# A new opening for a hypergraph block on one core: warm-up filled by VectorE, W2 prepared along its rows

## What is computed

```
H  = (adj != 0);  w = adj[:, 0, :]
Dn = 1 / (H @ w)          Be = 1 / (column sums of H)
conv(x, W, b) = Dn * (H @ (Be * (H^T @ (x @ W^T)))) + b
h   = relu(conv(x, W1, b1))            # 256 -> 512
h   = layer_norm(h) * gamma + beta
y   = conv(h, W2, b2) + x              # 512 -> 256
out = layer_norm(x + y)
```

## Time and profile before

| | |
|---|---|
| median of 3 runs | 283.41 us |
| profiled execution | 283.37 us, of which the span from first to last instruction is 281.6 us |
| TensorE (PE) busy | 273.6 us, 97% |
| VectorE (DVE) busy | 229.5 us, 82% |
| ScalarE (ACT) busy | 197.3 us, 70% |
| GpSimd (POOL) busy | 136.0 us, 48% |
| granted TensorE clock, mean | 0.995 |

### The profile page before, as it was taken

One profiled execution on the slowest core, in us unless ns is written; L12 is line 12 of the kernel. 1 busy time (PEld: TensorE's weight loads), 2 busy tenths in 40 slices (PEclk: granted clock), 3 DMA queues, 4 the chain that ended last, 5 costly groups with the idle time before them and its releaser, 6 DMA issues.

```text
span 281.6 us, 5797 instructions
## 1 busy us (share of the span) xinstructions
PE 273.6 (97%) x1820; PEld 249.5 (89%) x1820; DVE 229.5 (82%) x648; ACT 197.3 (70%) x561; POOL 136.0 (48%) x199
## 2 busy tenths in 40 slices
PE   7999999999999999999999999999999999999991
PEld 6889889898999989898998989899898989989891
DVE  3795689797878979797897979798897969798884
ACT  3588967776777787777768877676787765574723
POOL 2242546436363644536274553627355353637643
PEclk9999999999999999999999999999999999999998
DMA  6913041335324434432433533443333232110033
GB/s 213 328 55 84 3 130 40 93 113 132 115 57 133 92 93 117 130 114 64 147 72 94 137 109 112 63 147 52 100 91 95 77 113 74 40 57 21 1 112 112
DMA packets 37302, 27.70 MB, mean 98 GB/s; under 512 B 10060, under 2 KB 35352, under 8 KB 37272
## 3 DMA queue, kind: packets, MB, share of 16 engines
q1 hardware_dynamic: 37024, 27.17, 34.0%
q10 hardware_dynamic: 248, 0.17, 0.2%
HBM read 17.21 MB, written 8.42 MB: 91 GB/s over the span
## 4 chain that ended last, share of the span: by engine, by line
PE 90%; ACT 4%; DVE 3%; issue 1%; POOL 1%; POOLq 0%; DVEq 0%; ACTq 0%
PE bank_v L318 31%; PE bank_g L335 10%; PE bank_g L328 10%; PE bank_g L330 10%; PE bank_v L296 9%; PE bank_v L359 8%; PE bank_s L276 4%; PE bank_g L347 3%; PE bank_s L359 1%; PE bank_s L434 1%; ACT ht_sb L533 1%; ACT sq_sb L591 1%; PE bank_g L415 1%; DVE bn_sb L1000 1%; DVE w_lo L844 0%
## 5 line engine op out<-in xcount | busy, mean ns | idle before, releaser
L1049 POOL TENSOR_TENSOR xb_sb<-x_sb,b_half 128x512 f32<-128x512 f32 x32 | 41.2, 1291 | 69.6 <-DVE r_lo L774 50.1
L584 ACT ACTIVATE r_sb<-bank_v,vec 128x512 f32<-128x512 f32 x64 | 44.1, 689 | 39.5 <-PE bank_v L318 38.8
L328 PE MATMUL bank_g<-w_hi,r_hi 128*128 128x258 f32 x256 | 67.0, 294 | 0.0
L330 PE MATMUL bank_g<-w_lo,r_hi 128*128 128x256 f32 x256 | 63.7, 281 | 0.0
L1057 POOL TENSOR_SCALAR r_hi<-r_sb 128x512 fp32r<-128x512 f32 x64 | 44.0, 688 | 39.2 <-ACT r_sb L584 38.7
L318 PE MATMUL bank_v<-u_lo,w_hi 128*128 128x512 f32 x128 | 50.8, 397 | 0.0
L318 PE MATMUL bank_v<-u_hi,w_lo 128*128 128x512 f32 x128 | 50.8, 397 | 0.0
L318 PE MATMUL bank_v<-u_hi,w_hi 128*128 128x512 f32 x128 | 50.7, 396 | 0.0
L328 PEld LDWEIGHTS bank_g<-w_hi,r_hi 128*128 128x128 f32 x256 | 48.3, 189 | 1.7 <-DVE w_lo L844 0.3
L774 DVE TENSOR_TENSOR r_lo<-r_sb,r_hi 128x512 fp32r<-128x512 f32 x64 | 48.7, 782 | 0.9 <-POOL r_hi L1057 0.9
L330 PEld LDWEIGHTS bank_g<-w_lo,r_hi 128*128 128x128 f32 x256 | 48.2, 188 | 1.2
(11 more groups left out here) (127 smaller groups left out, 460.0 us busy)
## 6 DMA issues: line engine op xcount, KB each, us to landing
x_sb<-in_x_dram SPq DMA_DIRECT2D x16, 512.0 KB, 3.9
out_dram<-z_sb SPq DMA_DIRECT2D x14, 512.0 KB, 3.3
adj_sb<-in_adj_dram SPq DMA_DIRECT2D x15, 256.0 KB, 4.1
d_row<-d_rows SPq DMA_DIRECT2D x13, 256.0 KB, 3.5
w_raw<-in_L_gnn_W_dram SPq DMA_DIRECT2D x2, 512.0 KB, 4.8
out_dram<-z_sb SPq DMA_DIRECT2D x3, 256.0 KB, 2.1
adj_sb<-in_adj_dram SPq DMA_DIRECT2D x2, 128.0 KB, 2.3
turned_h<-h_sb SPq DMA_TRANSPOSE x13, 2.4
```

The lines of the kernel that those rows point to most:

```text
L328: pe.matmul(bank_g[:, n, 0:W2COLS], r_hi[:, i % 2, k, graph(n)], w2_hi[:, k], start=(k == 0), stop=False)
L330: pe.matmul(bank_g[:, n, 0:DOUT], r_hi[:, i % 2, k, graph(n)], w2_lo[:, k], start=False, stop=False, skip_group_check=True)
L584: nc.scalar.activation(r_sb[:, k], bank_v[:, k % 2], ACT.Relu, bias=vec[:, k:k + 1]).then_inc(relu_ready, 1)
L1049: nc.gpsimd.tensor_tensor(xb_sb[:, i % 2, part], x_sb[:, i % 3, part], b2_half[:, :].unsqueeze(1).to_broadcast([P, n, DOUT]), ALU.add).the ...
```

## The change

The text of the opening is rewritten; the loop from group 1 on is as before.

1. Warm-up: a tile `warm_b` is filled by VectorE's first instruction, and the warm-up is 22 matmuls of it with itself, which wait for that fill alone. Two more stand behind the first transposes of H, ten ahead of `make_first_s`.
2. W2: gamma comes in as a row for all partitions (a broadcast DMA), not as columns. GpSimd multiplies each half of W2's outputs by it, VectorE centres each half along its row (`bn_stats`, `bn_aggr`, subtract), TensorE turns it, ScalarE and VectorE split it. `scale_w2`, `sum_w2` and `split_w2` in one piece are gone.
3. c2: beta comes in as a row as well; GpSimd multiplies W2 by it, VectorE takes the mean and puts it on a diagonal, and two matmuls of 128 columns with `ones` make c2 in bank_q. This stands late: behind q of group 0 on GpSimd, around `split_u(1)` on VectorE, behind `make_g(0, 3)` on TensorE.
4. `make_g(0, 0)` and `make_g(0, 1)` become `make_first_g`, the two graphs side by side; `make_first_v` does the same with the first two chunks of v; `make_first_u` goes half by half.
5. Orders: x and adj of group 1 are loaded ahead of W2; `turn_q(0)` and `make_u(1)` come behind `make_g(0, 2)`; `make_s(2)` comes behind `make_v(1, 1)`; `make_d(2)`, `make_b(3)`, `add_b2(0, 1)`, `make_htb(3)` and `make_a(2)` move back.

```diff
-KEEP_WARM = 10
+KEEP_WARM = 2
...
             load_x(0)
             load_adj(1)
+            sp.dma_start(gamma_b[:, :], gamma.unsqueeze(0).to_broadcast([P, HID])).then_inc(gamma_in, 16)
+            for c in range(KD):
+                sp.dma_start(w2_raw[:, c], W2[c * P:(c + 1) * P, :]).then_inc(w2_high_in if c else weights_in[2], 16)
             load_adj(2)
             load_x(1)
+            sp.dma_start(beta_b[:, :], beta.unsqueeze(0).to_broadcast([P, HID])).then_inc(beta_in, 16)
...
+            def make_first_g():
+                pe.wait_ge(w2_hi_ready, KD)
+                for n in range(2):
+                    for k in range(KH):
+                        pe.wait_ge(r_hi_ready, k + 1)
+                        add(n, k, r_hi, w2_hi, W2COLS, first=(k == 0))
+                for k in range(KH - 1):
+                    pe.wait_ge(r_lo_ready, k + 1)
+                    for n in range(2):
+                        add(n, k, r_lo, w2_hi, W2COLS)
+                pe.wait_ge(w2_ready, KD)
...
+            def make_c2():
+                pe.wait_ge(diag_ready, KD)
+                pe.wait_ge(at_ready, 2)
                 for c in range(KD):
+                    mm = pe.matmul(bank_q[:, graph(c)], ones[:, :], c2_diag[:, c], start=True, stop=True)
+                mm.then_inc(c2_made, 1)
...
+            pe.wait_ge(warm_ready, 1)
+            keep_warm(WARM_UP)
             pe.wait_ge(consts_ready, 2)
             turn_first_h(0)
+            keep_warm(KEEP_WARM)
+            turn_first_h(1)
             pe.wait_ge(edges_in, 16)
             pe.transpose(bank_g[:, 0, 0:N], edge_rows[:, :], ident[0:N, 0:N]).then_inc(edges_turned, 1)
+            keep_warm(5 * KEEP_WARM)
             make_first_s(0)
+            make_first_s(1)
             turn_w1(0)
+            turn_first_a(0)
             turn_w1(1)
...
+            turn_first_a(1)
+            make_first_u()
+            turn_h(1)
+            make_first_v()
+            make_v(0, 2)
             turn_w2(0)
+            make_v(0, 3)
             turn_w2(1)
             make_s(1)
+            make_first_g()
...
                 make_g(i, 2)
                 if i == 0:
+                    turn_a(1)
+                    turn_h(2)
                     turn_q(0)
+                    make_u(1)
                     make_v(1, 0)
-                    make_s(2)
...
                 if i == 0:
+                    make_c2()
                     make_v(1, 1)
+                    pe.wait_ge(c2_ready, 1)
+                    make_s(2)
                 make_v(i + 1, 2)
                 make_v(i + 1, 3)
...
@@ ScalarE, group 0
             square(0, 3)
+            make_a(1)
+            read_at(1)
+            read_ht(2)
...
                 relu(i + 1, 1)
                 square(i + 1, 1)
                 if i:
                     normalise(i - 1, 0)
+                else:
+                    make_htb(3)
+                    make_a(2)
                 relu(i + 1, 2)
...
@@ VectorE
+            add_squares(0)
             make_h(3)
             make_b(2)
+            sum_beta(0)
 
             for i in range(LAST):
                 split_u(i + 1)
                 if i == 0:
-                    make_b(3)
-                    make_d(2)
+                    sum_beta(1)
...
+                else:
+                    read_c2()
                 read_g(i, 0)
+                if i == 0:
+                    make_b(3)
                 if i + 4 < G:
                     make_h(i + 4)
                 split_r(i + 1, 0)
...
                 read_g(i, 1)
+                if i == 0:
+                    make_d(2)
...
@@ GpSimd
+            for c in range(KD):
+                nc.gpsimd.tensor_tensor(w2_beta[:, c], w2_raw[:, c], beta_b[:, :], ALU.mult).then_inc(beta_scaled, 1)
...
                 split_r(i + 1, 0)
                 if i:
                     inverse_std2(i - 1)
+                else:
+                    add_b2(0, 1)
                 split_r(i + 1, 1)
                 inverse_std1(i, 1)
```

More of the change, by code:

```diff
@@ L340, in make_g, with add @@
                     mm.then_inc(last_g_made, 1)
+            def make_first_g():
+                def add(n, k, r, w, cols, first=False, last=False):
+                    return pe.matmul(bank_g[:, n, 0:cols], r[:, 0, k, graph(n)], w[:, k], start=first, stop=last,
+                                     skip_group_check=True)
+                pe.wait_ge(w2_hi_ready, KD)
[8 more added lines that the diff above has]
+                pe.wait_ge(w2_ready, KD)
+                for n in range(2):
+                    for k in range(KH):
+                        add(n, k, r_hi, w2_lo, DOUT)
+                pe.wait_ge(r_lo_ready, KH)
+                for n in range(2):
+                    mm = add(n, KH - 1, r_lo, w2_hi, W2COLS, last=True)
+                mm.then_inc(g_made, 1)
             def turn_q(i):
@@ L371, in add_last_xb, with keep_warm @@
                     pe.matmul(last_z[n], ident_2[:, :], xb_sb[:, 1, n], start=True, stop=False)
+            def keep_warm(times):
+                for _ in range(times):
+                    pe.matmul(bank_q[:, graph(0)], warm_b[:, :], warm_b[:, :], start=True, stop=True)
             def turn_w1(c):
@@ L377, in turn_w1, with turn_w2 @@
                 mm.then_inc(w1_turned, 1)
-            def turn_w2(half):
-                pe.wait_ge(weights_in[2], 16)
+            def turn_w2(c):
+                pe.wait_ge(w2_centred, c + 1)
                 pe.wait_ge(ht_ready, 1)
[L382 to L385, removed]
+                for k in range(KH):
+                    mm = pe.transpose(w2_turned_in[:, c, k], w2_g[:, c, graph(k)], ident[:, :])
                 mm.then_inc(w2_turned, 1)
@@ L409, in make_first_u @@
                 pe.wait_ge(x_in[0], 16)
-                for c in range(KD):
[L411 to L430, removed]
+                for half in range(2):
+                    for c in range(KD):
+                        if half:
+                            pe.wait_ge(at_ready, 1)
+                        else:
+                            pe.wait_ge(vec_ready if c else edges_ready, 1)
+                        for n in each(half):
+                            mm = pe.matmul(bank_g[:, c, graph(n)], x_sb[:, 0, n, graph(c)], at_sb[:, 0, n],
+                                           start=True, stop=True)
+                        if half:
+                            mm.then_inc(u_made, 1)
@@ new lines, in make_first_v, with add @@
+            def make_first_v():
+                def add(k, c, w, u, first=False, last=False):
+                    return pe.matmul(bank_v[:, k], w[:, c, graph(k)], u[:, c], start=first, stop=last,
+                                     skip_group_check=True)
+                pe.wait_ge(u_hi_ready, 1)
+                for k in range(2):
+                    pe.wait_ge(w1_ready, k + 1)
+                    add(k, 0, w1_hi, u_hi, first=True)
+                    add(k, 0, w1_lo, u_hi)
+                pe.wait_ge(u_lo_ready, 1)
+                for k in range(2):
+                    add(k, 0, w1_hi, u_lo)
+                pe.wait_ge(u_hi_ready, KD)
+                for k in range(2):
+                    add(k, 1, w1_hi, u_hi)
+                    add(k, 1, w1_lo, u_hi)
+                    pe.wait_ge(u_lo_ready, KD)
+                    add(k, 1, w1_hi, u_lo, last=True).then_inc(v_made, 1)
@@ L682, in _ @@
                 if i == 0:
[L683 to L691 removed]
+                    make_htb(2)
+                    read_ht(3)
+                elif i + 3 < G:
+                    make_htb(i + 3)
+                relu(i + 1, 0)
+                square(i + 1, 0)
                 relu(i + 1, 1)
@@ L1096, in _ @@
             pool.wait_ge(consts_ready, 5)
-            for k in range(KH):
-                split_r(0, k)
-            copy_w(2)
             for i in range(LAST):
@@ L1103, in _ @@
                     copy_w(i + 3)
-                for half in range(2):
-                    add_b2(i, half)
+                add_b2(i, 0)
+                if i:
+                    add_b2(i, 1)
                 inverse_std1(i, 0)
```

187 lines of the change are left out of this document (75 added, 112 removed).

## The result

The changed kernel takes **288.15 us** (median of 6 runs, 287.83 to 289.92); the kernel before took 283.40 us in the same comparison (6 runs, 283.37 to 283.72). The ratio is 1.0182 with a 95% interval of 1.0152 to 1.0211: slower by 4.75 us. The forecast was 285.1 us with a range up to 286.2, so the direction was right and the size was not.

The account below looks back on a forecast made before the run. TensorE was taken to bound the kernel, so only the start of make_g(1, 0) counts: 44.0 after two new stalls plus an unchanged 241.1 gives 285.1 us, own range 284.2 to 286.0, stated range 283.1 to 286.2.

Parts of the forecast that it names:

- The loop unchanged, 241.1 us: From make_g(1, 0) to the end the kernel takes 241.1 us as before, with only TensorE counting.
- The start and the way up to u(1): Opening on TensorE: make_first_s at 5.65, turn_first_a(0) at 7.6, make_v(0, 2) at 14.0, u(1) ending at 26.1.
- the warm-up doesn't cover: Rival, chance 0.05: TensorE still at 1.2 GHz at make_first_s, whose halves take 0.89 more: 286.0 us.
- W2 hidden, c2 without a wait: W2 complete at 10.8, its preparation covered by about 2 us; c2's two matmuls run without idle time before them.
- The first stall: TensorE idles 1.35 us ahead of v(1, 0), waiting for u_lo behind make_b(2) and sum_beta(0) on VectorE; start at 27.45.
- The second stall: TensorE waits ahead of turn_a(2) for the chain from c2 to make_a(2): idle 2.0 us at the near end.
- far end: Second stall with add_b2(0, 1) on GpSimd and r_lo on VectorE delaying each other by 0.8: turn_a(2) at 38.7, loop at 44.1.
- `turn_a(2)` to the loop, 5.4: make_g(1, 0) follows turn_a(2) by 5.4 us instead of 4.83, as y waits longer for ReLUs behind make_a(2).
- the gain stays: Rival, chance 0.10: both stalls covered, TensorE runs on from 26.1, loop starts at 40.0: 281.1 us.

Follow-up runs that it names:

- e1: The changed kernel with sum_beta(0) moved behind split_u(1) on VectorE: 286.77 us, 1.0109 of the kernel before.
- e5: The kernel of e4 with make_g(0, 2) put back between make_u(1) and v(1, 0) on TensorE: 283.01 us, 0.9977 of the kernel before.
- e12: The changed kernel with the edits of e1, e3, e5, e6 and e10 together: 282.24 us, 0.9954 of the kernel before.
- e10: The kernel of e5 with GpSimd's second product of W2 and beta waiting for make_b(2): 283.20 us, 0.9987 of the kernel before.
- e8: The changed kernel with unused warm-tile matmuls in both waits, 30 ahead of v(1, 0) and 45 ahead of turn_a(2): 286.65 us, 1.0116 of the kernel before.
- e6: The changed kernel with add_b2(0, 1) on GpSimd moved behind inverse_std1(0, 1): 287.01 us, 1.0112 of the kernel before.
- e4: The changed kernel with the edits of e1 and e3 together: 283.66 us, 1.0008 of the kernel before.
- e3: The changed kernel with make_d(2) on VectorE ahead of make_var1(0, 1) instead of behind read_g(0, 1): 286.33 us, 1.0078 of the kernel before.
- e2: The changed kernel with 30 unused warm-tile matmuls between make_u(1) and v(1, 0) on TensorE: 287.95 us, 1.0147 of the kernel before.
- e11: The changed kernel with the edits of e1, e3, e5 and e6 together: 282.17 us, 0.9942 of the kernel before.
- e9: The kernel of e5 with make_a(2) ahead of make_htb(3) on ScalarE: 283.93 us, 1.0024 of the kernel before.

## Why the prediction missed

The loop start was forecast at 44.0 and came at 47.13. By its steps:

- **The loop unchanged, 241.1 us:** right (47.13 + 241.1 = 288.2).
- **The start and the way up to u(1):** `make_first_s` came at 5.71 against 5.65, but its eight passes took 1.27 (to 6.98) instead of 0.89. VectorE waited for the first half's result until 6.73, where 6.25 had been reckoned, so `turn_first_a` was at 8.00 against 7.6. This is the rival "the warm-up doesn't cover" in part, 0.4 of its 0.89. The same opening had `turn_first_a` anywhere from 7.54 (e1, e5, e12) to 9.10 (e10) in the other profiles; 7.6 is the good end of that. The rest was sized a little short each time: `make_v(0, 2)` came at 14.62 against 14.0, and u(1) ended at 26.9 (its sixteen passes start at 25.10) against 26.1: **0.8**.
- **W2 hidden, c2 without a wait:** right, though W2 came later than the 10.8 assumed: GpSimd's first product waits for it until 11.71, and the cover took that up. (Ahead of W2 in the queue stand x of group 0 and adj of group 1; x of group 1 is loaded behind it.)
- **"The first stall", idle 1.35:** this is the step that failed. The mechanism was right: u_lo releases v(1, 0), and `sum_beta(0)` stands ahead of it. Two things in it were sized wrong. `make_b(2)` and the diagonal were taken as short steps, and took 0.39 and 0.75 beside GpSimd's work on b2: v(1, 0) started at 28.95 against 27.45, of which 0.8 is the late u(1): another **0.7**. And the idle time was priced as a plain wait. The clock fell behind it: six matmuls of v in 1.64 instead of 1.40, `make_g(0, 3)` in 2.58 instead of 1.44, c2 to its reading (34.06) in 0.89 instead of 0.6, together **1.7**. e8 shows that part by itself: 1.5 in the profiles, 1.5 to 1.8 in the times (0.1 of the v matmuls' 0.24 stands in e8 too, at a clock of 1.00). The prediction looked for a low clock at the start only, and gave no price to an idle TensorE in mid-opening.
- **"The second stall":** right, at its far end. From c2's reading (34.06) to `turn_a(2)` (41.69) 7.6 against 7.8, released by `make_a(2)`, which stands behind VectorE's dinv (40.30). e6 shows r_lo and `add_b2` as the pair. Only the parts are shared out differently: r_hi behind `add_b2` took 1.05 instead of 0.65.
- **`turn_a(2)` to the loop, 5.4:** right, 5.44.

0.8 + 0.7 + 1.7, less 0.2 of the second stall, is 3.0 of the 3.1 us; the rest is that the far end, 44.1, was taken as 44.0. The Trainium skill (TensorE: Matmul & The Clock Gate, "What's actually happening") was cited for the default low level at the start; the same passage has an idle array return to it. The traces here agree in part: in the change the granted clock was 1.00 before 1.80 us of idle time and 0.50 behind it, but it stayed at 1.00 behind the 2.63 ahead of `turn_a(2)`. In the prediction the return was left out.

The rival "the gain stays" (281.1) needed both waits covered. The kernel of e12 covers them and is at 281.93 in its profiled run: of the 0.8 that lack, 0.6 stand behind `turn_a(2)`, where the rival took the old 4.83 and e12 needs 5.45 (35.38 to 40.83). That the shared ports hold VectorE (the Trainium skill, SBUF — State Buffer, "Who interferes with whom") agrees with 1.78 against 0.68 for r_lo and 1.29 against 0.16 for four columns.

What stays open is the spread between runs of one kernel with the new opening. Part of it is how often the clock falls: the change's two longest runs (289.67 and 289.92) have the lowest mean clocks, 0.983 and 0.984. Another part lies in the start. e8's runs spread by 1.3 us with no fall in its profile. The two were not separated run by run: one run of the change at 0.994 took 288.1, which fewer falls alone don't explain.

## What to carry to other kernels

An idle time of TensorE has two prices, the wait and the clock that may fall at it; look for the second in the granted clock of short stretches, since the busy share stays at 1.00. With two waits of that kind, look at the other once one is gone: with the first cut to 0.52 us the clock fell at the second (e1), and only with both cut was the kernel back at 283.66 (e4). When work is moved onto GpSimd, see which VectorE operations then run beside it, small ones too: their durations from a quiet stretch don't hold there.

## What the runs showed of the hardware that was not expected

- The fall comes at different moments, and not each time. In the change TensorE idled until 28.95, worked at a clock of 1.00 to 30, and had 0.50 in 31 to 33; in e1 the clock fell in the idle time itself (0.90 in 38 to 39, the work from 39.16). It fell at waits of 1.80 (the change), 2.43 (e3) and 3.08 (e1), and did not in the profiles of 2.63 (the change's second wait, and e2's), 2.44 and 1.54 (e6). Waits of 0.81 and less (e4, e5 and e12) had none in their profiles.
- How VectorE's small operations meet GpSimd's differs between executions of one order. `make_b(2)` and the first diagonal took 0.39 and 0.75 in the change, where the first wait was 1.80, and 0.65 and 1.12 in e3 and e6, which leave that part as it is and waited 2.43 and 2.44.
- The start differs between executions too. In some the second half of adj lands later: VectorE waited 0.93 for it in e11's profile, and `make_first_s` took 2.04:

```profile
4.10 0.29 DVE L901 TENSOR_SCALAR h_sb<-adj_sb 128x256 bf16<-128x256 f32 x1 [0.93 <-DMA adj_sb<-in_adj_dram]
...
5.07 1.25 PE L403 MATMUL bank_s<-warm_b 128*128 128x128 bf16 x10
6.12 2.04 PE L428 MATMUL bank_s<-htb_sb,ht_sb 128*128 128x129 f32 x8
```

  In e8, e5 and e12 it took 1.37, with waits of 0.27 to 0.37 for that load. The landing alone doesn't decide it: e3 waited 0.30 and took 1.79. What goes with it in every profile of the new opening is the pace of the ten warm-up matmuls just ahead: 1.25 for the ten in the change, e3, e9, e10 and e11 (`make_first_s` 1.44 to 2.04), 0.73 to 0.87 in the others (1.37). The granted clock reads 1.00 in these microseconds in every profile, so at the start that column doesn't show the pace; what sets it stays open.
